# Two-layer graph attention plus masked multi-head attention on one core: the second projection in three fp16 terms, weight preparation in placed pieces, a new order

## The reference

```python
h = jnp.maximum(_layernorm(x, axis=-1), 0.0)
x = x + gat_two_layers(adj, h, W1, att_src1, att_dst1, b1, W2, ...)
h = jnp.maximum(_layernorm(x, axis=-1), 0.0)
x = x + mha(h, adj, Wq, Wk, Wv, Wo)     # 8 heads of 32, masked softmax, relu, Wo
# a gat_layer:
xl = (x @ W).reshape(B, N, H, F)         # layer 1: 4 heads of 128; layer 2: 1 head of 256
e = leaky_relu(asrc[:, :, None, :] + adst[:, None, :, :], 0.2)
attn = softmax(where(mask, e, -1e9), axis=1)
out = einsum('bsdh,bshf->bdhf', attn, xl) + bias     # elu after layer 1
```

## Time and profile before

| what | value |
|---|---|
| median of 3 runs | 776.16 us (776.13 to 776.79) |
| the profiled execution's own time | 774.69 us |
| its span in the trace | 772.6 us |
| busy PE, DVE, ACT, POOL | 716.3, 681.4, 591.6, 515.8 us |
| granted TensorE clock, mean | 0.989 |

### The profile page before, as it was taken

How to read it: one execution, slowest core, us unless ns; L and a number is a source line. 1 busy time by engine, 2 the same in 40 slices (tenths; PEclk the granted TensorE clock), 3 DMA queues, 4 the chain that set the end, 5 groups by cost and what they waited for, 6 DMA issues and landing times.

```text
span 772.6 us, 26496 instructions
## 1 busy us (share of the span) xinstructions
PE 716.3 (93%) x8398; PEld 593.4 (77%) x8398; DVE 681.4 (88%) x2017; ACT 591.6 (77%) x1865; POOL 515.8 (67%) x733
## 2 busy tenths in 40 slices
PE   0389999999999999999999999999999999999973
PEld 0157788888888888888888888888888888788852
DVE  4758899999999999999999999999999989999873
ACT  0167888888888778888888788788888888788752
POOL 5456777676767676667667766676677767766551
PEclk9999999999999999999999999999999999999996
DMA  6111555666578566557766656766655666655464
GB/s 197 33 37 43 106 112 112 121 110 118 118 117 115 116 112 113 119 114 115 122 110 118 112 124 115 115 110 120 114 119 116 113 119 106 112 118 105 89 110 89
DMA packets 270423, 84.70 MB, mean 110 GB/s; under 512 B 242896, under 2 KB 269904, under 8 KB 270288
## 3 DMA queue, kind: packets, MB, share of 16 engines
q1 hardware_dynamic: 270288, 83.02, 57.8%
HBM read 15.86 MB, written 8.39 MB: 31 GB/s over the span
## 4 chain that ended last, share of the span: by engine, by line
PE 75%; DVE 9%; DMA 5%; issue 4%; SPq 3%; ACT 1%; POOL 1%; DVEq 0%; ACTq 0%; POOLq 0%
PE bank L815 28%; PE bank L840 11%; PE bank L986 7%; PE bank L947 6%; DMA hT<-h_split 4%; PE bank L966 3%; PE bank L929 3%; PE bank L936 3%; PE bank L866 3%; PE bank L891 2%; PE bank L889 2%; PE bank L881 2%; SPq L276 1%; DVE top L756 1%; PE bank L874 1%
## 5 line engine op out<-in xcount | busy, mean ns | idle before, releaser
L497 ACT ACTIVATE e<-bank,nmx,q_power 128x128 f32<-128x128 f32 x512 | 194.7, 481 | 5.1 <-DVE nmx L761 5.1
L372 POOL CAST e_split<-e 128x512 f16<-128x512 f32 x128 | 82.4, 643 | 118.6 <-ACT e L497 118.6
L374 POOL TENSOR_TENSOR e_split<-e,e_split 128x512 f16<-128x512 f32 x128 | 151.7, 1185 | 10.3
L840 PE MATMUL bank<-w,h1T 128*128 128x258 f32 x512 | 122.8, 382 | 0.7 <-DVE shift L599 0.7
L386 POOL TENSOR_TENSOR rstd<-var,minus_half 128x1 f32<-128x1 f32 x128 | 71.7, 560 | 66.6 <-DVE var L625 66.6
L815 PE MATMUL bank<-w_split,hT 128*128 128x260 f16 x768 | 98.2, 278 | 12.3 <-DMA hT<-h_split 11.9
L840 PEld LDWEIGHTS bank<-w,h1T 128*128 128x128 f32 x512 | 96.6, 190 | 16.6 <-DVE h1T L655 1.6
L448 ACT ACTIVATE eT<-lr,nmx 128x128 f32<-128x128 f32 x256 | 102.7, 458 | 0.8 <-DVE nmx L713 0.8
L815 PE MATMUL bank<-h2T,proj_split 128*128 128x128 f16 x1536 | 97.4, 220 | 1.6 <-DMA h2T<-h_split 1.6
L815 PEld LDWEIGHTS bank<-h2T,proj_split 128*128 128x128 f16 x1536 | 92.0, 99 | 3.7 <-DMA h2T<-h_split 2.4
L815 PEld LDWEIGHTS bank<-w_split,hT 128*128 128x128 f16 x768 | 71.1, 98 | 24.5 <-issue 7.0
(11 more groups left out here) (116 smaller groups left out, 1921.7 us busy)
## 6 DMA issues: line engine op xcount, KB each, us to landing
x_in<-in_x_dram SPq DMA_DIRECT2D x64, 128.0 KB, 2.3
out_dram<-x_out SPq DMA_DIRECT2D x64, 128.0 KB, 2.0
adj_in<-in_adj_dram SPq DMA_DIRECT2D x64, 64.0 KB, 2.5
e3T<-e_split SPq DMA_TRANSPOSE x128, 3.1
hT<-h_split SPq DMA_TRANSPOSE x64, 2.4
h2T<-h_split SPq DMA_TRANSPOSE x64, 2.5
attT<-att_split SPq DMA_TRANSPOSE x64, 2.8
w<-in_L_gnn_W_dram SPq DMA_DIRECT2D x2, 256.0 KB, 3.1
```

Of the source, the lines that this page charges most:

```text
L372: pool.tensor_copy(e3_split[:, g.two, half, 0], e).then_inc(s[high_set], 1)
L374: pool.tensor_tensor(e3_split[:, g.two, half, 1], e, e3_split[:, g.two, half, 0], ALU.subtract).then_inc(s[low_set], 1)
L497: ins = act.activation(e3[:, g.two, h, :], S[:, h // 4, (h % 4) * N:(h % 4 + 1) * N], ACT.Exp, bias=nmx3[:, g.two, h:h + 1], scale=q_power ...
L840: ins = pe.matmul(X2[:, 0:D + 2], h1T[:, g.two, k * F:(k + 1) * F], w2[:, k, :], start=k == 0, stop=k == H - 1)
```

## The change

1. `project2` runs in three fp16 terms: `h1T` is split by ACT (`h1_high`, a copy to fp16) and POOL (`h1_low`, a subtraction), and `w2` is split once (`w2_scale`). Twelve fp16 matmuls take the place of eight fp32 ones. A power of two bounds h1, so the two evacuations and `elu` multiply by a scale that is read per partition.
2. Weight preparation is cut into pieces (`@once`, run for graph 0 only), each placed in the lists with a lag of its own. W1 is loaded first, and the three rows that belong to it go out from ACT's queue. Nothing waits in place for PE any more, except inside a piece.
3. The last three pieces of the diff are the lists of POOL, DVE and PE. All five lists have a new order and new lags (on PE 0 to 6 where they were 3 to 11), and the PSUM banks are given out anew, with the waits that go with it.

```diff
             def elu(g):
                 done(dve, s["ex_set"], g)
-                free(dve, s["x2_done"], g)
-                dve.scalar_tensor_tensor(out=h1T[:, g.two, :], in0=ex[:, g.two, :], scalar=1.0, in1=O1[:, :],
+                free(dve, s["h1_high"], g)
+                free(dve, s["h1_low"], g)
+                dve.scalar_tensor_tensor(out=h1T[:, g.two, :], in0=ex[:, g.two, :], scalar=h1_scale[:, 0:1], in1=O1[:, :],
...
+            def h1_high(g):
+                done(act, s["h1T_set"], g)
+                free(act, s["x2_done"], g)
+                act.activation(h1_split[:, g.two, 0, :], h1T[:, g.two, :], ACT.Copy).then_inc(s["h1_high"], 1)
...
+            def h1_low(g):
+                done(pool, s["h1T_set"], g)
+                done(pool, s["h1_high"], g)
+                free(pool, s["x2_done"], g)
+                pool.tensor_tensor(h1_split[:, g.two, 1, :], h1T[:, g.two, :], h1_split[:, g.two, 0, :], ALU.subtract).then_inc(s["h1_low"], 1)
...
             def project2(g):
-                done(pe, s["h1T_set"], g)
+                if g.n == 0:
+                    pe.wait_ge(s["w2_low"], 2)
+                done(pe, s["h1_high"], g)
+                done(pe, s["h1_low"], g)
...
-                if g.n == 0:
-                    w2_sums()
-                for k in range(H):
-                    ins = pe.matmul(X2[:, 0:D + 2], h1T[:, g.two, k * F:(k + 1) * F], w2[:, k, :], start=k == 0, stop=k == H - 1)
-                ins.then_inc(s["x2_done"], 1)
+                split_matmul(X2[:, 0:D + 2], [
+                    [(h1_split[:, g.two, i, k * F:(k + 1) * F], w2_split[:, j, k, :]) for i, j in SPLIT] for k in range(H)]).then_inc(s["x2_done"], 1)
...
-                dve.tensor_tensor(ab2[:, g.two, :], X2[:, D:D + 2], shift2[:, :], ALU.subtract).then_inc(s["ab2_set"], 1)
+                dve.scalar_tensor_tensor(out=ab2[:, g.two, :], in0=X2[:, D:D + 2], scalar=x2_power[:, 1:2], in1=shift2[:, :],
+                                         op0=ALU.mult, op1=ALU.subtract).then_inc(s["ab2_set"], 1)
...
-                dve.tensor_tensor(xl2[:, g.two, :], X2[:, 0:D], b2_all[:, :], ALU.add).then_inc(s["xl2_set"], 1)
+                dve.scalar_tensor_tensor(out=xl2[:, g.two, :], in0=X2[:, 0:D], scalar=x2_power[:, 0:1], in1=b2_all[:, :],
+                                         op0=ALU.mult, op1=ALU.add).then_inc(s["xl2_set"], 1)
...
-            for n in range(2):
-                sp.dma_start(x_in[:, n, :], x[n]).then_inc(x_here[n], 16)
             for k in range(KD):
                 sp.dma_start(w1[:, k, :, 0:HF // 2], W1[k * 128:(k + 1) * 128, :].rearrange("p (a c) -> p a c", a=2)).then_inc(s["w1_in"], 16)
-            for k in range(2):
-                sp.dma_start(att1[:, k, :], (att_src1, att_dst1)[k].rearrange("h f -> (h f)").partition_broadcast(128)).then_inc(s["w1_in"], 16)
-            sp.dma_start(b1_all[:, :], b1.partition_broadcast(128)).then_inc(s["w1_in"], 16)
+            for n in range(3):
+                sp.dma_start(x_in[:, n, :], x[n]).then_inc(x_here[n], 16)
...
+            for k in range(2):
+                act.dma_start(att1[:, k, :], (att_src1, att_dst1)[k].rearrange("h f -> (h f)").partition_broadcast(128)).then_inc(s["att1_in"], 16)
+            act.dma_start(b1_all[:, :], b1.partition_broadcast(128)).then_inc(s["b1_in"], 16)
...
             steps(lambda graphs: run([
-                (e3_last_halves, 9), (masks, 3), (e3_first_halves, 8), (rsqrt1, 2), (rsqrt2, 6), (diagonal2, 5),
-                (normalise, 4),
+                (h1_low, 9), (rsqrt2, 10), (split_low0, 9), (normalise, 8), (diagonal2, 9), (products_w2, 6), (masks, 3),
+                (products_w1, 1), (split_low3, 10), (e3_last_halves, 11), (split_low1, 9), (split_low2, 9), (rsqrt1, 4),
+                (picks, 0), (e3_first_halves, 11),
...
             steps(lambda graphs: run([
+                (residual2, 11), (gat1_scores, 5), (gat2_scores, 7), (relu1_low, 3), (att_norm, 10), (proj_scale, 6),
+                (ab_high, 4), (w1_scale, 3), (gat2_recip, 7), (ab_low, 4), (norm1_moments, 1), (proj_largest, 5), (xl_evac, 4),
+                (elu, 6), (att_low, 10), (residual1, 7), (qk_low, 8), (norm2_moments, 7), (w2_scale, 6), (variance2, 7),
+                (norm1_apply, 2), (w1_row, 2), (gat1_recip, 5), (w1_largest, 0), (w2_row, 5), (b1_prep, 3), (norm2_apply, 7),
+                (mha_max, 8), (ab2_evac, 6), (proj_row, 5), (relu2_low, 7), (w2_sums, 4), (w1_products, 0), (w1_sums, 1),
+                (w2_shift, 5), (variance1, 1), (xl2_evac, 6), (v_low, 8),
...
             steps(lambda graphs: run([
+                (turn_w1, 0), (spread_w1, 0), (project1, 0), (aggregate1, 2), (transpose2, 3), (transpose_ab, 0), (w2_ones, 1),
+                (qk, 4), (aggregate2, 3), (project_v, 4), (scores1_mask, 0), (scores3_mask, 4), (scores3_first, 4),
+                (scores1, 0), (turn_w2, 1), (scores3_last, 4), (turn_proj, 1), (project2, 2), (spread_w2, 1), (spread_proj, 1),
+                (project_out, 6), (transpose1, 1), (scores2, 2), (mha_av, 5),
```

More of the change, by code:

```diff
@@ L785, in _, with turn_w1 @@
+                (w2_shift, 5), (variance1, 1), (xl2_evac, 6), (v_low, 8),
+            ], graphs))
         @block.tensor
         def _(pe):
[L787 removed]
+            @once
+            def turn_w1(g):
                 pe.wait_ge(s["ident_set"], 5)
[L790 to L796 removed]
```

370 lines of the change are left out of this document (253 added, 117 removed).

## The result

| | before | changed |
|---|---|---|
| median of 4 runs, same chip | 776.14 us (775.66 to 776.79) | 855.74 us (853.85 to 857.79) |
| ratio | | 1.1025 (95% interval 1.0989 to 1.1061) |
| span of the profiled execution | 772.6 us | 855.9 us |

The change makes the kernel 10% slower. The forecast was 764 us with a range of 743 to 784: wrong in sign, and outside the range by 72 us.

What follows compares the result with a forecast made beforehand. PE bounded the kernel (10.86 us a step), DVE 0.3 us behind, taking over after the change. From the profiled 774.69 us: steps -1.9, start -10.2, drain 0 give 762.6; the runs' median 1.5 higher: 764 us, range 743 to 784.

Steps and rivals of the forecast that it cites:

- PE's floor falls from 10.86 to 10.46: Second projection on PE: twelve fp16 matmuls for eight fp32 ones take 0.40 us less per step.
- What DVE pays: DVE's two evacuations and elu, now with a scale: +0.14 us together, so DVE alone needs 10.69 us per step.
- What the order does to DVE: att_low on DVE falls into POOL's subtraction: +0.27 us, half of up to 0.55, making the step 10.96 us.
- The other collisions (apply 1, apply 2, low halves) I leave at what they cost now.: DVE's norm applies and low halves beside POOL: no added cost; norm2_apply could lose its collision, gaining up to 0.24 us.
- `rsqrt2` behind `h1_low`: On POOL, with DVE's norm2_apply waiting: halves and DVE's variance both take about 2.3 us from qk's end, no slack.
- The loop through PE, 10.85: Loop from transpose_ab through qk, DVE, POOL's diagonal2, scores2, mha_av, project1 and aggregate1 back: 10.85 us per step.
- `h2T` and `attT` have about 1 us.: Transposing transfers: h2T and attT go out about 1 us ahead of need.
- Start, -10.2: Weight preparation before the fourth projection: gain 10.2 us, bounds 5 and 14; first projection at 19 us, fourth at 47.6.
- third rival: Preparation late in its new place, fourth projection where it was, only the steps' 1.9 us remain: 774 us, chance 0.12.
- Drain, 0: From the last projection to the last store's input: change of 0 us, bounds -3 and +2.
- Locked out by POOL: Second rival: DVE instructions wait out POOL's on the shared port, step 11.44 us, 792 us in all, chance 0.20.
- POOL stays out of the way: First rival: att_low and norm2_apply miss POOL's instructions, PE's floor of 10.46 us holds, 740 us, chance 0.20.

Runs made afterwards that it cites:

- e9: Kernel before, old order, with the fp16 second projection (unit scales, later work one step later) and h1_low ahead of masks on POOL: 774.8 us, ratio 1.000.
- e12: e9 with norm1_transpose ahead of store in SyncE's list: 765.7 us, ratio 0.9885 against the kernel before.
- e1: Changed kernel with att_low writing zeros by a memset instead of the subtraction: 845.1 us.
- e4: Changed kernel with att_low moved behind variance2 on DVE and project_out behind transpose1 on PE: 861.1 us.
- e3: Changed kernel with mha_max ahead of norm2_apply in DVE's list: 831.6 us.
- e2: Changed kernel with project2 back to fp32 matmuls, h1_high and h1_low gone, the new order kept: 852.2 us.
- e11: Changed kernel with mha_max ahead of norm2_apply on DVE and the two loads ahead of e3_transpose_last on SyncE: 826.7 us.
- e6: Changed kernel with the two loads (adj, x_in) ahead of e3_transpose_last in SyncE's list: 853.2 us.
- e8: Changed kernel with adj[1] loaded right behind adj[0], ahead of the weights' bulk: 853.1 us.
- e10: e11 with att_low as a memset, its subtraction left out: 807.8 us.

## Why the prediction was wrong, by its own steps

- **"PE's floor falls from 10.86 to 10.46."** Not contradicted, and not reached. With `h1_low` placed well, 21 of 56 steps in e9 and 24 in e12 lie at 10.44 to 10.70 us, where 55 of 56 steps of the kernel before took 10.86 or more. The stage is worth its 0.40 only in the shortest of them; on average e12 keeps 0.21.
- **"What DVE pays": +0.14.** Near in size: 474 for 410 ns, 747 for 688, 213 for 149, in all +0.19 us. The sentence on top of it, that DVE takes over the bound from PE, is not shown: in e1 and e4 DVE was spared work and the step kept most or all of its length.
- **"What the order does to DVE": `att_low` +0.27.** The step that failed first. The upper bound of 0.55 was too low as well: a mean of +0.61, and a median of 1186 ns. I let it lose half of POOL's remaining time; the row shows it ending 0.27 us behind POOL's subtraction, having waited for all of it. The prediction had the evidence (1.24 us for a 0.41 us instruction) and took half of a bound for the value, on the argument that both orders of arrival fit the rows. In the repeated step it arrived behind POOL far more often than not: 35 of its 64 instructions took over 1.1 us, 11 under 0.6. The second apply took 1.12 us in nearly every step.
- **"The other collisions (apply 1, apply 2, low halves) I leave at what they cost now."** Wrong for apply 2. It had moved under `normalise` and took 1100 ns for 606, while apply 1 fell from 775 to 417; the swap of e3, which undoes the first, gave 18 to 24 us. Even a gain of 0.24 was held possible for it.
- **`rsqrt2` behind `h1_low`: "Nothing, but nothing is left over."** Right for the reason given: at 414.90 us POOL, done with `h1_low`, waited 0.57 us for the variance. And yet `norm2_apply` has a wait of 0.36 us there. e2 shows it without `h1_low`: the round from variance to `rstd` and back is in the order itself.
- **The loop through PE, 10.85.** The kind of loop was right, through `mha_max`, `mha_av`, `project1` and `aggregate1`; its length was not. In e11 a round of this kind took 11.53 and 11.83 us, by way of `xl2_evac` and the bank it shares with `mha_av`, which the prediction does not have. No transfer was in the loop either; in other steps of e11 one of 3.8 to 4.1 us (`h2T`) closed it, where the median had been 2.5.
- **"`h2T` and `attT` have about 1 us."** Too little for `attT`: 44 us of waiting in all, counted as nothing. e6 took 29 of them away and the step lost only 0.07, so in the changed kernel this loss lay behind another.
- **Start, -10.2.** It was +2.7 at the first projection and +1.1 at the fourth (58.90 us), which is the sign of the third rival (no gain at the start): it came true as well. Two sizes were wrong: W1 landed at 8.18 us where about 5 was taken, and the splits ran beside POOL's products. One wait was not seen, that for adj[1] (4.2 us, shown by e8).
- **Drain, 0.** +1.0 us.
- **The rivals.** "Locked out by POOL" has the right mechanism and sign, and priced it at 792 us. Its 11.44 counted `att_low` and the low halves; the low halves stayed at 439 ns, the apply was left out, and so were the rounds over queues, transfers and banks. "POOL stays out of the way" gave 740 for the changed kernel; in the old order e12 came to 766.
- Of the signs, "`att_low` well over 412 ns" came true, and it belonged to the second rival as much as to the forecast. "DVE busy over 95% of a step" did not: 94 and 95% in the two steps shown, 93% from 300 to 700 us.

In short: the step that failed is "What the order does to DVE": two instructions, not one, stand beside POOL, and they cost 0.61 and 0.49 us where 0.27 and nothing were counted (the first apply gave 0.36 back). Of the 77 us in the steps, 48 go in e10, which removes both and moves the loads; up to 16 of these (64 times 0.25 us) may be work left out. The other 30 or so lie in rounds over engine lists, a shared bank, SyncE's queue and the transfers, which the sum had at nothing; their shares stay open.

## What to carry to other kernels

When two engines share a port, list for each two-input instruction of POOL which of DVE's instructions will stand beside it, and put the ones that read PSUM there: e9 gained 23 us by moving one entry, e3 some 20. In a periodic schedule the same instructions tend to meet in every step (the second apply did so in all but a few of 64), so give a collision its full price and not a mean over arrivals. Before a reordering, follow each cycle from an engine's instruction through queues, bank waits and transfers back to the next graph's, with the range of transfer times in the trace and not the median alone: an instruction queued behind another graph's work closes a loop that did not exist. And read a chain over many steps: in e11 two steps pointed at one round, and the steps behind them at another.
